# Normalisations issued by VectorE instead of GpSimd, the rotary layers' scaling split between GpSimd and VectorE, and a reordered start-up

## What is computed

```python
def _layernorm(x, axis=-1, eps=1e-05):
    m = jnp.mean(x, axis=axis, keepdims=True)
    v = jnp.var(x, axis=axis, keepdims=True)
    return (x - m) / jnp.sqrt(v + eps)
...
x = x + jnp.tanh(g_xattn[0]) * _L0_xattn_ref(ctx_2048, _layernorm(x, axis=-1), ...)
x = x + jnp.tanh(g_ffn[0]) * _L0_ffn_ref(_layernorm(x, axis=-1), ...)
...
x = x + jnp.tanh(g_ffn[3]) * _L3_ffn_ref(_layernorm(x, axis=-1), ...)
```

```python
q, k, v = jnp.split(h @ wqkv, 3, axis=-1)
q = l2norm(q) * qs
k = l2norm(k) * ksc
q, k = rotary_xpos(q, k)
o = local_attention(q, k, v)
```

## Time and profile before

| what | value |
|---|---|
| median of three runs | 1534.86 us |
| lowest, highest | 1533.13 us, 1537.53 us |
| time of the profiled execution | 1534.07 us |
| its span, first to last instruction | 1532.3 us |
| mean granted clock of PE | 0.969 of full speed |
| PE, DVE busy | 88%, 86% of the span |
| ACT, POOL busy | 68%, 58% of the span |

### The profile page before, as it was taken

How to read it: one execution, slowest core, us unless ns; L and a number is a source line. 1 busy time by engine, 2 the same in 40 slices (tenths; PEclk the granted TensorE clock), 3 DMA queues, 4 the chain that set the end, 5 groups by cost and what they waited for, 6 DMA issues and landing times.

```text
span 1532.3 us, 42104 instructions
## 1 busy us (share of the span) xinstructions
PE 1342.6 (88%) x16024; PEld 942.2 (61%) x16078; DVE 1313.8 (86%) x3926; ACT 1036.3 (68%) x2051; POOL 882.5 (58%) x1402
## 2 busy tenths in 40 slices
PE   3788899998998898988988998998899998987977
PEld 2556666666666675666665666666656576665644
DVE  4787899888988999889898889898889988898777
ACT  1355678766766777776766777767776776776556
POOL 5865764566645766476576466566556546565230
PEclk9799999999999999999999999999999999999969
DMA  7002201111101221111111112011211012110020
GB/s 226 9 15 53 63 17 43 32 44 45 46 21 30 57 57 23 42 37 46 33 32 48 41 43 53 21 34 40 63 26 47 8 46 49 41 33 24 18 66 7
DMA packets 133592, 64.38 MB, mean 42 GB/s; under 512 B 98442, under 2 KB 124170, under 8 KB 133137
## 3 DMA queue, kind: packets, MB, share of 16 engines
q1 hardware_dynamic: 131953, 57.08, 14.8%
q10 hardware_dynamic: 1440, 4.60, 0.8%
HBM read 50.06 MB, written 2.14 MB: 34 GB/s over the span
## 4 chain that ended last, share of the span: by engine, by line
PE 35%; DVE 24%; POOL 17%; ACT 12%; issue 7%; DMA 2%; POOLq 2%; SPq 1%; DVEq 0%; another core or an unknown queue 0%
PE ps_all L1489 6%; POOL wide_a L643 5%; POOL rden L643 4%; PE ps_all L1774 4%; POOL rstd L643 4%; POOL y L796 3%; DVE mx L1171 3%; ACT L870 3%; PE ps_all L1527 3%; PE ps_all L1553 3%; PE ps_all L1482 3%; DVE wide_b L1174 2%; PE ps_all L1566 2%; DVE wide_b L1228 2%; PE ps_all L1612 2%
## 5 line engine op out<-in xcount | busy, mean ns | idle before, releaser
L643 POOL TENSOR_TENSOR rstd<-rstd,minus_half 128x1 f32<-128x1 f32 x320 | 194.2, 610 | 361.6 <-DVE rstd L1156 360.3
L643 POOL TENSOR_TENSOR rden<-rden,minus_half 128x16 f32<-128x16 f32 x64 | 188.7, 2948 | 9.4
L1171 DVE TENSOR_REDUCE mx<-ps_all 128x8 f32<-128x512 f32 (+1 forms) x192 | 164.8, 861 | 26.1 <-PE ps_all L1515 9.4
L643 POOL TENSOR_TENSOR wide_a<-wide_a,wide_b 128x256 f32<-128x256 f32 x256 | 180.4, 737 | 1.7 <-DVE wide_b L1228 1.6
L908 ACT COPY wide_a<-ps_all 128x512 f32<-128x512 f32 (+1 forms) x192 | 139.0, 727 | 57.4 <-PE ps_all L1489 30.8
L1489 PE MATMUL ps_all<-ident,wide_b 128*128 128x128 f32 x1024 | 154.6, 284 | 22.3 <-ACT wide_b L921 16.4
L870 ACT ACT_TABLE_LOAD x129 | 165.5, 1283 | 2.3
L1489 PEld LDWEIGHTS ps_all<-ident,wide_b 128*128 128x128 f32 x1024 | 118.4, 145 | 56.9 <-issue 21.0
L921 ACT ACTIVATE wide_b<-wide_b 128x512 f32<-128x512 f32 (+1 forms) x160 | 114.3, 716 | 42.8 <-DVE wide_b L1174 41.5
L908 ACT COPY wide_c<-ps_all 128x128 f32<-128x128 f32 (+2 forms) x192 | 94.7, 498 | 60.8 <-PE ps_all L1489 35.1
L1482 PE MATMUL ps_all<-ident,y 128*128 128x128 f32 x320 | 93.4, 311 | 44.7 <-POOL y L796 26.6
(11 more groups left out here) (261 smaller groups left out, 3619.2 us busy)
## 6 DMA issues: line engine op xcount, KB each, us to landing
wide_c<-wide_c SPq DMA_DIRECT2D x128, 64.0 KB, 2.2
wide_a<-in_k SPq DMA_DIRECT2D x32, 256.0 KB, 2.6
wide_a<-in_k SPq DMA_DIRECT2D x64, 128.0 KB, 2.6
v_pad<-in_v SPq DMA_DIRECT2D x64, 128.0 KB, 2.9
wide_c<-in_v SPq DMA_DIRECT2D x32, 136.0 KB, 2.7
ctx_t<-in_ctx_t SPq DMA_DIRECT2D x29, 128.0 KB, 2.8
ctx_s<-in_ctx SPq DMA_DIRECT2D x29, 128.0 KB, 3.1
out<-x SPq DMA_DIRECT2D x32, 64.0 KB, 1.8
```

The lines of the kernel that those rows point to most:

```text
L643: return gp.tensor_tensor(o, a, b, op)
L1171: v.tensor_reduce(most, of, AX.X, ALU.max).then_inc(*done(f"{n}_max"))
```

## The change

**Normalisations.** The five `y` instructions of a tile move from POOL to DVE; POOL keeps the power. DVE now waits for POOL's power before each.

**Scaling.** DVE's one instruction of 1024 columns becomes one of 512 columns for the keys. POOL gets a new stage `qn` behind its own additions: two instructions of 256 columns, for the queries. PE transposes the keys' four pieces first and waits for `qn` ahead of the queries' four.

**Start.** ACT waits for the small bias and mask loads before it issues the ternary weights. It then waits for the first weights, computes the gates, issues three of the nine further arrays, sums the absolute values of the ternary weights in four instructions of its own, and issues the other six arrays. DVE's sum (L1068) goes.

**Tables.** `ORDER` and `BANK_TABLE` are new throughout. Both are left out here but for a line each.

```diff
     "pool": """
-        l0a_rstd l0a_y l0a_part l0f_rstd l0f_y l0f0n_rstd l0f0_rot l0f0_one l0f0_rstd l0f1n_rstd l0f1_rot
-        l0f1_one l0f1_rstd l1a_rstd l1a_y l1f_rstd l2a_rstd l2a_y l2f_rstd l2f_xb l3a_rstd l3a_y l3f_rstd
+        l0a_rstd l0a_part l0f_rstd l0f0n_rstd l0f0_rot l0f0_qn l0f0_one l0f0_rstd l0f1n_rstd l0f1_rot l0f1_qn
+        l0f1_one l0f1_rstd l1a_rstd l1f_rstd l2a_rstd l2f_rstd l2f_xb l3a_rstd l3f_rstd
...
-l0f0_qkt 06163115431610002563123005146526 2 l0f0_qts
+l0f0_qkt 26062113431620143563023104145026 2 l0f0_qts
...
-                def normalise(n, of):
-
-                    yield f"{n}_y"
-                    tile(f"{n}_rstd")
-                    gp.tensor_scalar(y[:, s, :], of[:, s if of is x else i % EARLY, :], mv[:, s, 0:1], rstd[:, s:s + 1], ALU.subtract,
-                                     ALU.mult).then_inc(*done(f"{n}_y"))
...
+                    yield f"{n}_qn"
+                    tile(f"{n}_rot")
+                    tile(f"{n}n_rstd")
+                    for k in range(2):
+                        part = slice(256 * k, 256 * k + 256)
+                        n_op = tt(wide_b[:, s, part].rearrange("p (g e) -> p g e", g=4),
+                                  wide_a[:, s, part].rearrange("p (g e) -> p g e", g=4),
+                                  bc(rden[:, s, 4 * k:4 * k + 4], 2, ROW), ALU.mult)
+                    n_op.then_inc(*done(f"{n}_qn"))
...
+            act.wait_ge(signal("bias_in"), 48)
             act.dma_start(raw, d["tern"]).then_inc(signal("tern_in"), 16)
-            for to, of in soon:
-                act.dma_start(to[:], of).then_inc(signal("weights_soon"), 16)
             act.wait_ge(signal("weights_now"), NOW)
             a.activation(gate[:], gate_in[:], ACT.Tanh).then_inc(signal("gates"), 1)
+            for to, of in soon[:3]:
+                act.dma_start(to[:], of).then_inc(signal("weights_soon"), 16)
+            act.wait_ge(signal("tern_in"), 16)
+            for n, dump in enumerate((w_conv[:, 0, :], w_conv[:, 1, :], w_conv[:, 2, :], tern[:, 0, :])):
+                m = a.activation(dump, raw[:, n, :], ACT.Abs, accum_out=tern_sum[:, n:n + 1])
+            m.then_inc(signal("tern_rows"), 1)
+            for to, of in soon[3:]:
+                act.dma_start(to[:], of).then_inc(signal("weights_soon"), 16)
...
-            dve.wait_ge(signal("tern_in"), 16)
-            v.tensor_reduce(tern_sum[:], raw, AX.X, ALU.add, apply_absolute_value=True)
-            v.drain().then_inc(signal("tern_rows"), 1)
...
+                def normalise(n, of=None):
+
+                    yield f"{n}_y"
+                    tile(f"{n}_rstd")
+                    ts(y[:, s, :], x[:, s, :] if of is None else of, mv[:, s, 0:1], rstd[:, s:s + 1], ALU.subtract,
+                       ALU.mult).then_inc(*done(f"{n}_y"))
...
-                    tt(wide_b[:, s, :].rearrange("p (g e) -> p g e", g=16),
-                       wide_a[:, s, :].rearrange("p (g e) -> p g e", g=16),
-                       bc(rden[:, s, :], 2, ROW), ALU.mult).then_inc(*done(f"{n}_qkn"))
+                    tt(wide_b[:, s, BANK:2 * BANK].rearrange("p (g e) -> p g e", g=8),
+                       wide_a[:, s, BANK:2 * BANK].rearrange("p (g e) -> p g e", g=8),
+                       bc(rden[:, s, 8:16], 2, ROW), ALU.mult).then_inc(*done(f"{n}_qkn"))
...
-                    for c in range(8):
+                    for c in (4, 5, 6, 7, 0, 1, 2, 3):
+                        if c == 0:
+                            tile(f"{n}_qn")
                         m = nc.tensor.transpose(ps(f"{n}_qkt", c * P, P), wide_b[:, s, c * P:c * P + P], ident[:])
```

More of the change, by code:

```diff
@@ L127 @@
+        vuvtutvvuuttvuvu
         """,
     "act": """
[L129 to L133 removed]
@@ L816, in chain @@
                 yield from inv_std("l0f")
-                yield from normalise("l0f", x)
                 for L in range(2):
@@ L848, in chain @@
                 yield from inv_std("l3a")
-                yield from normalise("l3a", x)
                 yield from inv_std("l3f")
@@ L1284, in chain @@
                 yield from above_zero("l0a")
+                yield from normalise("l0a", xin[:, e, :])
                 yield "l0a_k"
@@ L1303, in chain @@
                 yield from above_zero("l0f")
+                yield from normalise("l0f")
                 for L in range(2):
@@ L1309, in chain @@
                 yield from above_zero("l1a", LN_EPS * LN_EPS / (1.0 + LN_EPS))
+                yield from normalise("l1a")
                 yield from update("l1a", 1)
@@ L1349, in chain @@
                 yield from above_zero("l2a")
+                yield from normalise("l2a")
                 yield from scores64("l2a")
@@ L1376, in chain @@
                 yield from above_zero("l3a")
+                yield from normalise("l3a")
                 yield "l3a_part"
```

310 lines of the change are left out of this document (154 added, 156 removed).

## The result

The changed kernel takes 1529.04 us (median of 11 runs, 1524.38 to 1535.86), the kernel before 1535.6 us (11 runs on the same chips). The ratio is 0.9955 with a 95% interval of 0.9937 to 0.9974: **faster by 0.45%, about 7 us**. The forecast was 1541 us with a range of 1517 to 1556. The range holds the time, but the sign is wrong: faster had a chance of 0.31, slower 0.40.

A forecast was written before the change was run, and what follows sets the result against it. It took two nearly full engines as the bound, PE ahead of DVE by 28.8 us. Added DVE time +12.0, PE's waits -3.0, scaling 0 and start -3 made +6.0 on 1534.86 us: 1541 us, range 1517 to 1556.

The forecast's parts named there:

- The moved normalisations: On DVE, 160 instructions at 0.39 us add 62.4 us; POOL loses 134.9 us.
- The split: Halving DVE's scaling takes 34.0 us off DVE and adds 81.5 us to POOL; booked 0, with -4 and +6 as ends.
- POOL has room: POOL, 58.7% busy in the middle stretch, can take the queries' scaling and would end at 829 us busy, 54%.
- PE's waits: At the transposes of y, PE waits 19 us instead of 26.6, 7.6 less, booked as -3.0 us.
- The added wait: DVE idles for POOL's power before each y, 160 x 0.105 = 16.8 us of new idle time.
- DVE's weight, 0.28: A microsecond of added DVE work lies on the chain that ended last with weight 24/86 = 0.28.
- The start: Biases land some 3 to 5 us sooner and later weights move up: -3 us, with -6 and +3 as ends.
- the shorter hop counts: Rival: DVE takes each y at once, shortening POOL's links on the chain, -11 us to 1524 us; chance 0.28.
- DVE becomes the bound: Rival: DVE's busy time plus new idle, 1357 us, passes PE's 1343, giving 1553, up to 1572 us; chance 0.07.
- the long holding: Rival: POOL instructions hold new DVE ones for their whole length, 38 us more on DVE, 1551 us; chance 0.03.
- Signs of being wrong: DVE's y idling under 5 us and PE's under 10 (faster), or PE's middle-stretch busy share below 89.5% (slower).

The follow-up runs named there:

- experiment 3: Traced eps-to-power times, and moved only qn in POOL's row: right behind its additions in t_both, 1551.5 us; behind waiting powers in b_both, 1547.5 us.
- t_none: Kernel before with only the new ORDER and BANK_TABLE, normalisations on POOL, scaling one DVE instruction, old start: 1564.0 us, ratio 1.0201.
- b_y: Kernel before with its own tables and start, only the normalisations moved to DVE: 1533.5 us, ratio 0.9970.
- t_y: New tables and old start, normalisations moved to DVE, scaling still one DVE instruction: 1536.1 us, ratio 1.0001 to the kernel before.
- t_split: New tables and old start, queries' half of the scaling on POOL, normalisations still on POOL: 1567.8 us, ratio 1.0204 to the kernel before.
- t_both: Changed kernel with the old start, so new tables and both moves: 1521.7 us, ratio 0.9921 to the kernel before.
- b_split: Kernel before with its own tables and start, only the queries' half of the scaling moved to POOL: 1590.0 us, ratio 1.0339.
- b_both: Kernel before with its own tables and start, both moves made: 1563.1 us, ratio 1.0170.

## Why the forecast went wrong

- **The moved normalisations**, the instruction: right. 0.38 us for x and 0.36 for xin against 0.39 booked. 60.2 us against 62.4.
- **The split**, DVE's side: 52.3 us are left of 79.3, so 27.0 went instead of 34.0. The half's median is 0.69 us, as interpolated (0.706), its mean 0.817. It now runs at the same time as POOL's half, and that is new (below).
- **POOL's row and the new tables. This is the step that failed.** The forecast held that "POOL has room". It booked 0 for POOL's side of the split, with -4 and +6 as ends, and let the missing `y` instructions repay what `qn` holds up. It put no price on the queue that the leaving `y` shorten. And it gave `ORDER` and `BANK_TABLE`, which decide what stands behind `qn`, no term at all. The runs show in its place that time in POOL's row costs even at 54% busy (131 us of padding, +24 us in the new order), and that the place of `qn` alone is worth 24 us in the new order and 18 in the old one. The missing `y` do shorten the way from eps to power by 46 us in sum in the old order, but `qn` puts 84 us back (experiment 3). The new tables are worth 38 us to this assignment, and this missing term is what turns the sign.
- **In the forecast's terms:** it had the normalisations at +19 (DVE's 62.4 and 16.8 us at 0.28, less 3.0 for PE's waits). Measured: -4.6 in the old order, -31 or -43 in the new one. It had the split at -9.5 (34.0 us at 0.28, and 0 for POOL). Measured: +31 in the old order, +0.4 or -12 in the new one.
- **The added wait**: 9.2 us in 20 places instead of 16.8. Right in kind, half in size.
- **PE's waits**: 14.2 us for `y`, where 19 were expected and 26.6 stood before.
- **DVE's weight, 0.28**: measured 0.18 in the old order (0.05 to 0.30) and 0.45 in the new (0.27 to 0.62). DVE's busy time rose by 18.0 us and not by 26.1. Its durations rose by 37 us in sum, but records that follow each other closely overlap in the trace, and only their union is busy time. That also made the number booked and the number compared with it two different things.
- **The start**: -3 booked with +3 as the upper end, +5 measured. The biases came even earlier than forecast, the first PE work in the range named, and neither bought anything.
- **The rivals**: "the shorter hop counts" had the right side and 1524 us. It named the way of `y`, which is about half of the 43 us. The other half, POOL's queue, stood in no rival, although POOL's 17% of the chain at 58% busy hinted that an engine far from full can hold others up. "DVE becomes the bound" didn't come (its upper end, 1572, is also 3 us short of its own sum, 1534.9 + 43 - 3). Nor did the long holding: the slowest of the 160 new instructions took 0.827 us.

Terms in their order, for the record: both moves in the old order +26, the new order -38, the new start +5, together -7. The forecast had +9, 0 and -3. That the time still lies in the range is luck: errors of +17, -38 and +8 us cancel for the most part.

## What to carry over

On an engine that works through a fixed row and makes small things that others wait for, an added instruction can cost by what it holds up behind it, even when the engine is half idle. 24 us here hung on whether some 1.4 us of work stood right behind its additions or, in 36 of 64 places, later, mostly behind another tile's power. So price a moved instruction by the row it is moved into, and where a change replans that row, give the replanning a term of its own. The moves alone (+26 us) and the new order alone (+31 us) both lose here, together they gain 12.

A weight taken from the chain gives a size and no more: the chain read 0.28 and 0.30 in two orders in which added DVE work cost 0.18 and 0.45.

Signs of being wrong should cover the terms that were booked at nothing. Here they watched only the terms that had a number, and none of them fired.

## What was not expected of the hardware

**The two halves of the scaling get into each other's way.** This is DVE's half in the changed kernel, shortest, median and longest in ns:

```profile
L1244 DVE TENSOR_TENSOR wide_b<-wide_a,rden x64: 643/691/1136, 66.9 to 1414.7; 128x512 f32<-128x512 f32 x64
```

Both halves wait for the same additions, so where `qn` stands right behind these they start nearly together. The mean, 0.817 us, lies 0.13 us above the median. The undivided instruction's lies 0.02 us above (1.238 and 1.220 in the kernel before). 24 of the 64 halves take 0.83 us or more, and each of them began while a two-tensor instruction of POOL was running. The duration follows POOL's lead: 1.135 us where POOL's 0.61 us instruction had begun 0.02 us earlier, 0.994 at 0.17, 0.868 at 0.29, and 0.68 to 0.70 where it had begun 0.45 us earlier or more. That is what waiting for its end would give. It also goes the other way: POOL's next instruction, begun during DVE's held half, takes 1.06 us instead of 0.61. The Trainium skill (SBUF — State Buffer, "Who interferes with whom") says that a VectorE instruction with two SBUF inputs contends with a GpSimd instruction that reads SBUF. The trace agrees for this pair, 1.135 us against a median of 0.691. It doesn't agree for POOL's power of 2.95 us: the six halves that began inside one took 0.643 to 0.684 us, and the four new `y` instructions that did took at most 0.344.

The small power is held in its turn. Before, the slowest of the 320 took 1.63 us against a median of 0.557, and DVE's undivided scaling of 1.2 us began just behind its start. With the scaling halved, the slowest takes 1.09 us. The power's mean is 0.603 to 0.610 us in the four traces with the undivided scaling (before, t_none, b_y, t_y) and 0.560 to 0.569 in the five with the half (changed kernel, t_split, t_both, b_split, b_both). The forecast didn't book this, and no run shows what it is worth.

**The orders with more waits also have a lower granted clock.** PE executes the same 16078 instructions in 1342.8 us in t_both (mean granted clock 0.980), in 1360.9 us in b_both (0.965), and in 1375.4 us in b_split (0.953). The clock stands at the lower of its two levels, 1.2 and not 2.4 GHz, for 61 us of t_both's span, 108 of b_both's and 149 of b_split's. PE had been waiting more than usual ahead of its 20 falls between 60 and 1450 us in b_split: 55% busy in the last 5 us, against 86% over the span. Of the 73 us between the spans of t_both and b_split, 33 are PE's own busy time, with not an instruction added. So part of what a wait costs can come back as a slower PE. How much of the 33 us is the clock isn't shown by a run of its own.
